# A graph layer on one core: SyncE too fetches single rows for one tile of every twelfth group

## What is computed

```python
m_in = concat([x[src], x[dst], edge_attr], axis=-1)        # 400000 x 144
h = silu(m_in @ W1 + b1)
messages = silu(h @ W2 + b2)
agg = segment_sum(messages, dst, num_segments=12500)
out = layernorm(x + silu(concat([x, agg], axis=-1) @ W3 + b3))
```

## Time and profile before

| | |
|---|---|
| runs, us | 4507.25, 4509.8, 4517.8 (median 4509.8) |
| span of the profiled execution, us | 4497.7 |
| PE busy | 3654.5 us (81%) |
| DVE busy | 2757.0 us (61%) |
| POOL busy | 2591.6 us (58%), 2744 gathers |
| ACT busy | 1046.2 us (23%) |
| mean granted PE clock | 0.918 of full |
| mean DMA traffic | 33 GB/s |

### The profile page before, as it was taken

How to read it: one execution, slowest core, us unless ns; L and a number is a source line. 1 busy time by engine, 2 the same in 40 slices (tenths; PEclk the granted TensorE clock), 3 DMA queues, 4 the chain that set the end, 5 groups by cost and what they waited for, 6 DMA issues and landing times. The chain is left out here.

```text
span 4497.7 us, 68074 instructions
## 1 busy us (share of the span) xinstructions
PE 3654.5 (81%) x19180; PEld 2747.4 (61%) x19180; DVE 2757.0 (61%) x4834; ACT 1046.2 (23%) x1714; POOL 2591.6 (58%) x2754
## 2 busy tenths in 40 slices
PE   1588888888888888888888888888888888888888
PEld 1366666666666666666666666666666666666665
DVE  2366666666666666666666666665665666666667
ACT  0222222222222222222222222222222222222223
POOL 7365655556555655656555555555555555555650
PEclk6789999999999999999999999999999999999998
DMA  4211111111111111111111111111111111111110
GB/s 100 59 29 34 32 28 34 33 34 29 34 33 28 34 34 30 32 28 39 28 34 28 35 32 28 33 33 33 28 33 34 28 33 28 34 32 28 38 23 11
DMA packets 335197, 150.34 MB, mean 33 GB/s; under 512 B 224958, under 2 KB 290527, under 8 KB 334822
## 3 DMA queue, kind: packets, MB, share of 16 engines
q0 software_dynamic: 87808, 90.09, 9.5%
q1 hardware_dynamic: 237238, 54.50, 5.7%
q10 hardware_dynamic: 9776, 1.37, 0.2%
HBM read 136.10 MB, written 9.62 MB: 32 GB/s over the span
## 5 line engine op out<-in xcount | busy, mean ns | idle before, releaser
L547 POOL DMA_INDIRECT edge_in<-in_x_dram,src_i x2744 | 2590.4, 944 | 1789.7 <-issue 743.5
L1165 PE MATMUL pick_ps<-parts,rows_T 128*128 128x512 f32 (+1 forms) x9100 | 2298.7, 405 | 564.0 <-issue 268.6
L1165 PEld LDWEIGHTS pick_ps<-parts,rows_T 128*128 128x128 f32 x9100 | 1698.8, 196 | 993.7 <-issue 384.4
L646 ACT ACTIVATE z_ps<-z_ps,zero_col 128x512 f32<-128x512 f32 x391 | 258.9, 662 | 2859.1 <-DVE z_ps L855 1975.8
L855 DVE TENSOR_TENSOR z_ps<-z_ps,b_rep 128x512 f32<-128x512 f32 x391 | 272.4, 697 | 920.9 <-remote 553.3
L1099 PEld LDWEIGHTS in_ps<-ident,edge_in 128*128 128x128 f32 x3128 | 347.7, 144 | 362.1 <-issue 341.6
L1126 PEld LDWEIGHTS z_ps<-w_bd,h_T 128*128 128x128 f32 x3128 | 471.4, 219 | 145.6 <-DVE pair L878 82.8
L1126 PE MATMUL z_ps<-w_bd,h_T 128*128 128x128 f32 x3128 | 485.7, 306 | 81.0 <-DVE pair L878 61.1
L1120 PE MATMUL z_ps<-in_T,w_in 128*64 128x512 f32 x782 | 441.2, 646 | 19.8 <-issue 14.1
L1099 PE MATMUL in_ps<-ident,edge_in 128*128 128x128 f32 x3128 | 442.4, 286 | 13.9 <-issue 7.7
L1121 PE MATMUL z_ps<-in_T,w_in 128*64 128x512 f32 x782 | 442.4, 649 | 8.6 <-issue 8.5
(11 more groups left out here) (104 smaller groups left out, 1231.5 us busy)
## 6 DMA issues: line engine op xcount, KB each, us to landing
edge_in<-in_x_dram ACTq DMA_DIRECT2D x3968, 0.2 KB
edge_in<-in_x_dram,src_i POOLq DMA_INDIRECT x2744
ea<-in_edge_attr_dram SPq DMA_DIRECT2D x48, 512.0 KB
w_in<-node_terms SPq DMA_DIRECT2D x391, 12.0 KB
node_terms<-h_T SPq DMA_DIRECT2D x12, 256.0 KB
node_terms<-lot_T SPq DMA_DIRECT2D x12, 256.0 KB
y<-in_x_dram SPq DMA_DIRECT2D x15, 192.0 KB
term<-node_terms SPq DMA_DIRECT2D x15, 192.0 KB
```

The lines of the kernel that those rows point to most:

```text
L547: pool.indirect_dma_start(out=edge_in[:, to_slot, t, XS], out_offset=None, in_=x[:, :], in_offset=bass.IndirectOffsetOnAxis(ap=indices[:, ...
L1165: last = nc.tensor.matmul(pick_ps[at % PICK_BANKS][:, 0:(b - a) * H], rows_T[:, n % ROW_SETS, c, :], parts[:, j, a:b, :].rearrange("p k f ...
```

## The change

SP fetches one tile as well, in the groups with g % 12 == 6 from 30 to 378 (30 groups). POOL gathers one tile less there. SP loads the group's 128 indices in step g - 16 and fetches the rows in nine parts, in steps g - 12 to g - 4: 15 rows in each of the first eight and 8 in the last, right after the step's window load. PE waits for these rows before it transposes the group. Four pairs of semaphores serve in turn.

```diff
+    SP_EVERY, SP_AT, SP_SETS = 12, 6, 4
+    SP_PARTS = 9
+    SP_ROWS = -(-P // SP_PARTS)
+
+    def sp_fetched(g):
+        return g % SP_EVERY == SP_AT and 2 * S <= g < BODIES * B
+
+    SP_OF = {g: n for n, g in enumerate(g for g in range(FULL) if sp_fetched(g))}
...
+    SP_INDICES_OF = {g - S - 4: g for g in SP_OF}
 
     def tiles_of(g):
-        return TT if g == FULL else T - picked(g) - fetched(g)
+        return TT if g == FULL else T - picked(g) - fetched(g) - sp_fetched(g)
...
+            sp_row_regs = [sp.alloc_register(f"sp_row{i}") for i in range(SP_ROWS)]
+
+            def load_sp_indices(g):
+                sp.dma_start(sp_row_i[0:1, SP_OF[g] % 2, :], src_v[g:g + 1, :, fetched_tile(g)],
+                             allow_slow_non_contiguous=True).then_inc(s_sp_row_i[SP_OF[g] % 2], 16)
+
+            def fetch_sp_rows(g, part):
+                n = SP_OF[g]
+                rows = range(part * SP_ROWS, min(part * SP_ROWS + SP_ROWS, P))
+                if part == 0:
+                    sp.wait_ge(s_sp_row_i[n % 2], n // 2 * 16 + 16)
+                    sp.nop(nofuse=True)
+                sp.load(sp_row_regs[0:len(rows)], sp_row_i[0:1, n % 2, rows.start:rows.stop])
+                for reg, r in zip(sp_row_regs, rows):
+                    of = sp.snap(reg, min_val=0, max_val=N - 1)
+                    sp.dma_start(edge_in[r:r + 1, g % S, fetched_tile(g), XS],
+                                 x[bass.ds(of, 1), :]).then_inc(s_sp_fetched[n % SP_SETS][r % 2], 16)
...
                     load_window(k * B + (u + NW), u % NW)
+                    if k * B + u in SP_INDICES_OF:
+                        load_sp_indices(SP_INDICES_OF[k * B + u])
+                    for part in range(SP_PARTS):
+                        if sp_fetched(k * B + u + S - part):
+                            fetch_sp_rows(k * B + u + S - part, part)
...
+                if sp_fetched(v):
+                    for odd in range(2):
+                        pe.wait_ge(s_sp_fetched[SP_OF[v] % SP_SETS][odd], (SP_OF[v] // SP_SETS + 1) * (P // 2 * 16))
                 transpose_tiles(v % S).then_inc(s_in_T, 1)
```

More of the change, by code:

```diff
@@ L139, in fetched @@
         return g % S == 0 and 2 * S <= g < FULL
+    SP_EVERY, SP_AT, SP_SETS = 12, 6, 4
[4 more added lines that the diff above has]
+    SP_OF = {g: n for n, g in enumerate(g for g in range(FULL) if sp_fetched(g))}
+    assert not any(fetched(g) and sp_fetched(g) for g in range(FULL)) and SP_PARTS <= S - 1
     def fetched_tile(g):
@@ L201, in gnn_layer @@
         row_i = sb("row_i", [1, 2, P], I32)
+        sp_row_i = sb("sp_row_i", [1, 2, P], I32)
         base_i = sb("base_i", [1, Q * P], I32)
@@ L275, in gnn_layer @@
         s_row_i = [sem(f"row_indices_loaded{j}") for j in range(2)]
+        s_sp_row_i = [sem(f"sp_row_indices_loaded{j}") for j in range(2)]
+        s_sp_fetched = [[sem(f"sp_rows_fetched{j}_{o}") for o in range(2)] for j in range(SP_SETS)]
         s_fetched = [[sem(f"rows_fetched{j}_{o}") for o in range(2)] for j in range(2)]
```

## The result

| | before | after |
|---|---|---|
| median of 4 runs, us | 4508.5 (4486.5 to 4517.8) | 5137.2 (5105.5 to 5146.0) |
| span of the profiled execution | 4497.7 | 5103.7 |
| busy PE / DVE / ACT / POOL | 81 / 61 / 23 / 58% | 72 / 54 / 20 / 50% |
| mean granted PE clock | 0.918 | 0.868 |

The ratio is 1.139 (95% interval 1.134 to 1.144): the change makes the kernel 13.9% slower, and the time lies far outside the forecast's range of 4468 to 4575. The profiled run of the changed kernel took 5105.5 us, 1.8 more than its span; so what lies around a span is 1.8 us (in every other profiled run too), and most of the 12.1 us that I carried over was spread between runs.

A forecast was written before the change was run, and what follows sets the result against it. POOL's cycle of gathers and pauses was taken to pace the kernel. Span 4497.7 - 23 (POOL's relief) + 8 (ACT's delay) = 4483 us, with 12.1 us carried over 4495 us; range 4468 to 4575.

The forecast's parts named there:

- the 12.1 us that I carried over: Difference between the earlier kernel's median of runs, 4509.8, and its profiled span, added to the forecast span of 4483 us.
- What bounds the kernel: On POOL: its cycle of gathers and pauses paces the kernel, about 10.9 us a group of seven, though nobody waits for its data.
- the removal: On POOL: six gathers in place of seven in 30 groups take 37.6 us off its cycle, of which 23 arrive.
- the 0.6: Share of POOL's saved 37.6 us taken to arrive, as three of five neighbouring groups of six gathers were shorter.
- SP at nothing: On SP: bursts of 8.3 to 15.2 us fit into its idle time and cost the kernel nothing.
- the threshold: On SP: below 13.8 us a burst, PE would not have to wait for SP's rows.
- The row price: On SP: 0.41 us a row in a quick burst, 0.87 in a slow one, taken from ACT's rows.
- The register load: On SP: 15 registers at 0.063 us each, 1.15 us a burst, from ACT's load of 12 and SP's of one.
- The window load in front: On SP, before each burst: about 1.0 us from its register load to its transfer's end.
- the cover: On SP: 2639.8 us of waiting at one line, so bursts cost nothing while the backlog stays below some 33 us.
- SP itself is late: Rival: at 15.2 us a burst PE waits 11 us in 30 groups, about 4700 us with catching up; chance 0.07.
- ACT at +8: On ACT: rows slowed by SP's delay its silu beyond POOL's next release; 8 us taken, bounds 0 and 84.

The follow-up runs named there:

- e12_every24: The changed kernel with SP fetching its tile in every 24th group (15 groups), all else the same; 4833.7 us, ratio 1.075 to the kernel before.
- e5_fixed: The changed kernel with SP's row transfers reading fixed rows, without register load and register operation; 4537.9 us against 4506.7 for the kernel before, ratio 1.009.

## Why the prediction was wrong, point by point

**What bounds the kernel, and the removal: right.** POOL's cycle paces it although nobody waits for its rows; 30 tiles less were worth 25 us (forecast 23, bounds 0 to 37.6). That the two numbers are so close is partly luck, as the 0.6 came from five groups. The distance of some 1.6 us from POOL's last gather to ACT's start is common but not constant: over the run it is 1.4 to 1.9 us in 44% of the groups, with a median of 1.9.

**SP at nothing: the step that failed.** The working had the bounds (8.3 to 15.2 us a burst), the threshold (13.8) and the consequence. Counted as there, with the window load, the measured burst is 16.5 us: above the threshold and above the upper bound too. The choice between the ends was wrong, and no row spoke for it: I took nothing, with a chance of 0.07 for SP being late. Four terms made it so. The row price: the quick burst of the earlier trace rows was ACT's and began right at a release, when rows are quick; SP's fifteen come after a window and a load and run past POOL's fourth gather, and each late burst begins where rows are slow. The mean of 0.81 is next to the slow burst's 0.87, not to 0.41. The register load: 2.28 us in the mean for fifteen and not 1.15, since a price per register was taken from ACT's aligned loads; with aligned ones and a step more PE's waits fall by 42%, the time by 278 us. I set the Trainium skill's figure aside with a row that didn't test it. The window load in front: 2.0 us from its start to the register load and not 1.0, partly because other loads of SP stand between them. And the cover: SP's long waits were read as room for the backlog, but they are spread over all steps, while the deadline applies in nine of them; e12_every24 has 2072 us of such waits and loses 335 us.

**The price of the rival "SP itself is late" was half.** It gave PE 11 us in 30 groups, 4700; it waits 22.8. Bursts lengthen as they slide into slow stretches: the seventh takes 18.3 us in the mean, and the last two start some 48 us behind PE's z matmuls of their step where I had 33.

**ACT at +8: too small.** 0.028 us a row would be 108 us for 3840 rows, above the bound of 84; e5_fixed, with quicker SP rows, has 56. By this estimate the change would have taken 4540 to 4592 us even had SP kept up. The signs are those of the mechanism named: "issue" before L646 and POOL's waits for PE rise and "remote" doesn't. That ACT's own rows make the delay is not shown, since 529.9 us of "issue" stand there without any. In the change itself "issue" fell to 683.7, I think because ACT gets time while PE waits for SP.

**Sum with the measured terms:** 4509 - 25 + 108 + 30 x 19.8 = 5186, against 5137. The last two may overlap; no run parts them.

**What can't be settled.** Why reports and rows are late in most of the sets and in one are not. The program is the same, the chip was the same one at least once, and POOL's gathers are as long and closer together where rows are quick, so the gathers alone aren't the cause, although within a 4500 us run rows slow with them. What the change itself does under the conditions of 3467 us wasn't met: its two neighbours gained 0.6 and 0.85% there.

## What to carry to other kernels

An engine that idles half of the run can still be too slow for a burst with a deadline: divide the burst by the step in which it stands, at the price of its last instructions, and add what is queued behind it. Take the price from rows that start at the same place in the cycle, and where the bounds straddle the threshold, let the chance say so. Where an engine loads many registers at once, let the load begin at a multiple of 16 bytes.

## What was unexpected of the hardware

- A load of 15 registers from SBUF takes 1.39 us from a start at a multiple of 16 bytes and 3.08 from another (0.205 a register); 16 aligned take 0.98.
- Where the kernel takes 4500 us, SP's row transfers are 0.44 us apart in POOL's first gather of a group and 1.7 to 1.9 from the fifth on, and are quick at once (0.43) when POOL stops.
- The same kernel took 3467 us in one set of runs and 4497 to 4534 in the others, each set steady within 0.7%, once both on the same chip. In the first, POOL's pauses of 2.5 us for late reports are absent.
- Where the kernel takes 4500 us, row transfers beside POOL's gathers cost the kernel an estimated 0.013 us (ACT's) to 0.03 us (SP's) each with nobody waiting for them.
